# A state-space scan and an FFN on one core: drives on GpSimd and TensorE, decays in SBUF, weighing split between GpSimd and VectorE

## What is computed

```python
x = x + ssm(ctx, layernorm(x), ...)
x = x + ffn(layernorm(x), ...)

def ssm(hidden, z, ...):
    x = einsum('ed,bld->bel', in_proj_w, hidden)
    u = silu(causal_conv4(x) + conv_b)
    dt_lo, Bm, Cm = split(einsum('ke,bel->bkl', x_proj_w, u))
    delta = softplus(dt_proj_w @ dt_lo + dt_proj_b)
    A = -exp(A_log)
    def step(state, ...):                       # over the 256 time steps
        state = state * exp(delta[..., None] * A) + (delta * u)[..., None] * B[:, None, :]
        y = einsum('ben,bn->be', state, C)
    y = (y + D * u) * silu(z)

def bit_linear(x, w, b):                        # the FFN's three products
    x_q = round(x * 127 / max|x|) ; w_q = clip(round(w / mean|w|), -1, 1)
ffn = bit_linear(silu(bit_linear(x, gate)) * bit_linear(x, val), out)
```

## Time and profile before

| | |
|---|---|
| three runs | 226.61, 226.84, 227.04 us (median 226.84) |
| span of the profiled execution | 224.8 us |
| what lies around the span | some 2.0 us (median less span) |
| first scan | 26.94 us |
| last weighing ends | 186.84 us |
| first scan to last weighing | 159.9 us |
| behind the last weighing | 38.0 us |

### The profile page before, as it was taken

One profiled execution on the slowest core, in us unless ns is written; L12 is line 12 of the kernel. 1 busy time (PEld: TensorE's weight loads), 2 busy tenths in 40 slices (PEclk: granted clock), 3 DMA queues, 4 the chain that ended last, 5 costly groups with the idle time before them and its releaser, 6 DMA issues.

```text
span 224.8 us, 2405 instructions
## 1 busy us (share of the span) xinstructions
PE 150.9 (67%) x706; PEld 92.9 (41%) x706; DVE 186.5 (83%) x284; ACT 129.3 (58%) x197; POOL 136.8 (61%) x132
## 2 busy tenths in 40 slices
PE   6983088643979197059630777926986667899983
PEld 5531054232636186048620533504435265334552
DVE  3789999998089999999999968797869998838661
ACT  2578675336585996076341758736498015376772
POOL 5036499778900999896685999999139202691000
PEclk9995559978585769758785596985589969999999
DMA  4894943261400223004003304314000000000002
GB/s 107 231 343 123 339 146 112 87 189 42 140 13 0 75 66 92 4 0 141 0 0 98 135 3 136 73 71 140 23 1 3 23 0 0 0 28 0 23 23 70
DMA packets 12689, 17.44 MB, mean 78 GB/s; under 512 B 3468, under 2 KB 9012, under 8 KB 12678
## 3 DMA queue, kind: packets, MB, share of 16 engines
q1 hardware_dynamic: 12678, 17.30, 24.5%
HBM read 16.11 MB, written 1.19 MB: 77 GB/s over the span
## 4 chain that ended last, share of the span: by engine, by line
DVE 19%; PE 16%; ACT 9%; issue 6%; POOL 5%; DVEq 0%; POOLq 0%; ACTq 0%
DVE wstate L908 3%; PE work L1242 2%; DVE state L898 2%; PE work L1282 2%; DVE gam L981 2%; DVE xhat L825 2%; PE decay L1067 2%; ACT decay L653 2%; DVE pool_state L898 2%; DVE wstage L976 2%; POOL drive L491 2%; ACT gT L722 2%; ACT wstage L703 1%; PE decay L1242 1%; PE work L1249 1%
## 5 line engine op out<-in xcount | busy, mean ns | idle before, releaser
L491 POOL TENSOR_TENSOR drive<-du,b_wide 128x1024 f32<-128x1024 f32 x31 | 74.2, 2407 | 2.9 <-DVE state L898 1.8
L653 ACT ACTIVATE decay<-delta,aneg 128x510 f32<-128x510 f32 x64 | 42.9, 684 | 45.9 <-DVE state L898 23.3
L898 DVE TENSOR_TENSOR_SCAN state<-decay,drive 128x512 f32<-128x512 f32 x44 | 52.4, 1208 | 0.9 <-issue 0.9
L1156 PE MATMUL ysum<-ident,wstate 128*128 128x128 f32 x176 | 32.9, 332 | 10.6 <-DVE wstate L908 10.6
L908 DVE TENSOR_TENSOR wstate<-state,cwide 128x512 f32<-128x512 f32 x44 | 29.1, 663 | 12.2 <-issue 11.8
L1156 PEld LDWEIGHTS ysum<-ident,wstate 128*128 128x128 f32 x176 | 26.1, 172 | 18.8 <-DVE wstate L908 13.8
L501 POOL TENSOR_TENSOR pool_wstate<-pool_state,c_wide 128x1024 f32<-128x1024 f32 x10 | 23.7, 2367 | 11.4 <-PE ysum L1156 8.6
L898 DVE TENSOR_TENSOR_SCAN pool_state<-decay,drive 128x512 f32<-128x512 f32 x20 | 24.3, 1214 | 0.2 <-ACT decay L653 0.2
L1067 PE MATMUL work<-ident,wstage 128*128 128x128 f32 x80 | 14.2, 331 | 11.4 <-ACT ternary L677 7.7
L1177 PE MATMUL cwide<-cparts,sel 128*128 128x512 bf16 x22 | 10.6, 483 | 15.4 <-DVE wstate L908 14.2
L1067 PEld LDWEIGHTS work<-ident,wstage 128*128 128x128 f32 x80 | 11.8, 174 | 12.7 <-ACT ternary L677 8.1
(11 more groups left out here) (180 smaller groups left out, 298.7 us busy)
## 6 DMA issues: line engine op xcount, KB each, us to landing
b_wide<-bc_rows SPq DMA_DIRECT2D x16, 512.0 KB, 4.5
c_wide<-bc_rows SPq DMA_DIRECT2D x10, 256.0 KB, 3.5
x_in<-in_x SPq DMA_DIRECT2D x2, 512.0 KB, 4.9
wstage<-in_L_ffn_gate_w SPq DMA_DIRECT2D x1, 1024.0 KB, 7.8
wstage<-in_L_ffn_val_w SPq DMA_DIRECT2D x1, 1024.0 KB, 10.3
wstage<-in_L_ffn_out_w SPq DMA_DIRECT2D x1, 1024.0 KB, 9.0
ctx_in<-in_ctx SPq DMA_DIRECT2D x2, 256.0 KB, 4.4
out<-wtap SPq DMA_DIRECT2D x4, 128.0 KB, 1.7
```

What stands on the lines that cost most here:

```text
L491: nc.gpsimd.tensor_tensor(drive[:, m % NDR], du[:, m // NS], rows.unsqueeze(1).to_broadcast([P, EH, W]), ALU.mult).then_inc(s_drive, 1)
L653: nc.scalar.activation(v[:, :, 1:L], d[:, :, 1:L], ACT.Exp, scale=aneg[:, eh, n:n + 1]).then_inc(s_decay, 1)
L898: nc.vector.tensor_tensor_scan(dst, decay[i % ND][:], drive[:, i // EH % NDR, i % EH], 0.0, ALU.mult, ALU.add).then_inc(s_scan, 1)
L1156: last = nc.tensor.matmul(ysum[:, k, eh * P:(eh + 1) * P], lhsT=src[:, k * P:(k + 1) * P], rhs=ident[:], start=start and k % LB == 0, stop ...
```

## The change

Almost the whole scan part is written anew; the FFN's products stay.

- The unit of work is a *slot*: a pair of neighbouring states (`NP = 8` pairs a group) of one half of the channels, for both batches. There are 32 slots. Each has two scans, one for each batch, of two states x 256 steps, so again 64 scans of 512 columns.
- `decays` writes SBUF (four slots of buffers), in two activations of 510 columns a slot.
- The drive of three pairs (`DIAG_PAIRS`, 6 slots) comes from TensorE: du is turned (`turn_du`, `duT`), GpSimd writes B on diagonals with an affine select (`diagonals`, `bdiag`), and two fp32 matmuls of 256 columns for each scan put du x B into a PSUM bank. The drive of the other thirteen pairs (26 slots) is a GpSimd multiplication of 1024 columns into SBUF (`pool_drive`, two buffers), two slots ahead.
- C is spread over the partitions by a DMA for every pair (`c_wide`); `spread_c` and `split_c` go. VectorE weighs the 12 slots of `DVE_SLOTS`, GpSimd the other 20, one instruction of 1024 columns each.
- The matrix of the delta projection is multiplied out ahead (`wdT`), so that `pre_delta` needs no copied projection. TensorE adds the parts of softplus (`add_delta`) for three of the four halves. The D x u term is a matmul with a diagonal (`ddiag`).
- silu(layernorm(x)) is one ScalarE activation with scale and bias, turned by TensorE afterwards. The ternary clip is ScalarE's Sign in `weight_rows`; `clip_weights` goes. The two additions of x behind the gate move from GpSimd to VectorE. `scales` is one instruction shorter.
- ctx of group 0 is loaded from ScalarE's queue.

```diff
-NDR = 4
-ND = 3
-POOL_C = (2, 5, 8, 13, 17, 19, 21, 24, 26, 28)
+ND = 4
+NDRV = 4
+NST = 3
+NPW = 2
+NCW = 3
+NBW = 2
+NPD = 2
+DIAG_PAIRS = (0, 1, NP)
+DVE_SLOTS = (3, 5, 7, 9, 11, 13, 15, 17, 19, 21, 23, NSLOT - 1)
+POOL_LEAD = 2
...
+            def load_c(k):
+                if k >= NCW:
+                    for s in slots_of(k - NCW):
+                        wait_weighed(sp, s)
+                sp.dma_start(c_wide[:, k % NCW]..., on_all(1, k)).then_inc(s_cload[k % NCW], 16)
...
+            def diagonals(k):
...
+                nc.gpsimd.affine_select(out=bdiag[:, r % NDG]..., in_=values.unsqueeze(2).to_broadcast([P, GT * 2, P]),
+                                        compare_op=ALU.is_equal, fill=0.0, ...).then_inc(s_diag, 1)
+            def drive_slot(s):
...
+                if r >= NPD:
+                    pool.wait_ge(s_scan, BG * [j for j in range(s) if not on_diag(j)][r - NPD] + BG)
...
+                nc.gpsimd.tensor_tensor(pool_drive[:, r % NPD], rows, b_wide[:, w % NBW], ALU.mult).then_inc(s_pdrive, 1)
+            def weigh(s):
...
+                nc.gpsimd.tensor_tensor(flat(pool_wstate[:, r % NPW]), flat(state[:, s % NST]), flat(c_wide[:, k % NCW]),
                                         ALU.mult).then_inc(s_poolw, 1)
...
+            for s in range(NSLOT):
+                for k in DIAG_PAIRS[2:]:
+                    if s == slots_of(k)[0] - DIAG_LEAD:
+                        diagonals(k)
+                if s + POOL_LEAD < NSLOT and not on_diag(s + POOL_LEAD):
+                    drive_slot(s + POOL_LEAD)
+                if s not in DVE_SLOTS:
+                    weigh(s)
+                if s == POOL_XRSTD:
+                    rstd(0)
...
+                nc.scalar.activation(decay[:, s % ND, :, n, 1:L], d[:, :, 1:L], ACT.Exp,
+                                     scale=aneg[:, eh, 2 * p + n:2 * p + n + 1]).then_inc(s_decay, 1)
...
             def scan(i):
...
+                if on_diag(s):
+                    dve.wait_ge(s_drive, BG * r + b + 1)
+                    rows = drive[(BG * r + b) % NDRV][:]
+                else:
+                    dve.wait_ge(s_pdrive, r + 1)
+                    rows = pool_drive[:, r % NPD, b].rearrange("p n l -> p (n l)")
...
+                nc.vector.tensor_tensor_scan(state[:, s % NST, b]..., decay[:, s % ND, b]..., rows, 0.0,
                                              ALU.mult, ALU.add).then_inc(s_scan, 1)
...
+                nc.vector.tensor_tensor(flat(wstate[:]), flat(state[:, s % NST]), flat(c_wide[:, k % NCW]),
                                         ALU.mult).then_inc(s_wst, 1)
...
+            for i in range(NUNIT):
                 scan(i)
+                if i % BG == BG - 1 and i // BG in DVE_SLOTS:
+                    weigh(i // BG)
+                if i in DVE_XVAR:
+                    k = DVE_XVAR.index(i)
+                    dve.wait_ge(s_x[k // 2], 16)
+                    bn(x_in, 2 * k, 2 * k + 2, s_var if k == 3 else None)
...
+            def drives(i):
...
+                for c in range(LB):
+                    t = b * LB + c
+                    last = nc.tensor.matmul(bank[:, :, c * P:(c + 1) * P], lhsT=duT[:, g, t, eh], rhs=bdiag[:, d % NDG, t],
+                                            start=True, stop=True)
```

More of the change, by code:

```diff
@@ L52 @@
 BROWS = VROW + PARTS * PARTS
[L56 to L68, removed]
@@ L89, in sums_at @@
[L89 to L95, removed]
+NP = NS // 2
+SLOTS = NP * EH
+UNITS = SLOTS * BG
+ORDER = [(0, 0), (1, 0), (0, 1), (1, 1)] + [(p, eh) for p in range(2, NP) for eh in range(EH)]
+NSLOT = G * SLOTS
+NUNIT = G * UNITS
+ND = 4
+NDRV = 4
+NST = 3
+NPW = 2
+NDG = 2
+NCW = 3
+NBW = 2
@@ new lines, with slot_of, slot_parts, slots_of @@
+TURNS, WARM = (6, 6), (16, 3)
+def slot_of(g, p, eh):
+    return g * SLOTS + ORDER.index((p, eh))
+def slot_parts(s):
+    g, k = divmod(s, SLOTS)
+    p, eh = ORDER[k]
+    return g, p, eh
+def slots_of(k):
+    return sorted(slot_of(k // NP, k % NP, eh) for eh in range(EH))
+def pair_of(s):
+    g, p, _ = slot_parts(s)
+    return g * NP + p
+def on_diag(s):
+    return pair_of(s) in DIAG_PAIRS
+def drive_rank(s):
+    return sum(on_diag(k) == on_diag(s) for k in range(s))
+def wide_rank(k):
+    return sum(j not in DIAG_PAIRS for j in range(k))
@@ L1122, in convolve_tap, with pre_delta @@
                     fill(last, name)
+            def pre_delta(g, eh):
+                name = f"pre{g}{eh}"
+                t = work_tile(name)
+                if g == 0:
+                    wait_read(pe, "wd")
+                for k in (1, 0):
+                    wait_u(pe, g, k)
+                    last = nc.tensor.matmul(t[:], lhsT=wdT[:, k, eh * P:(eh + 1) * P], rhs=u[:, k], start=k == 1,
+                                            stop=k == 0)
+                fill(last, name)
             def project(g):
-                name = f"proj{g}"
+                name = f"bc{g}"
                 t = work_tile(name)
@@ L1143, in gates, with turn_b @@
-            def gates(k):
-                name = f"z{k}"
-                t = work_tile(name)
-                pe.wait_ge(s_xhat, LB * (k + 1))
+                for k in (1, 0):
+                    wait_u(pe, g, k)
+                    last = nc.tensor.matmul(t[0:2 * NS, :], lhsT=bcT[:, k], rhs=u[:, k], start=k == 1, stop=k == 0)
+                fill(last, name)
+            def turn_b(g):
+                name = f"bt{g}"
+                t = work_tile(name)
+                wait_read(pe, f"bc{g}")
+                for k in range(GT):
+                    last = turn(t[:, k * NS:(k + 1) * NS], proj[0:NS, k * P:(k + 1) * P])
+                fill(last, name)
@@ new lines, in turn_du, with skips @@
+            def turn_du(g, eh):
+                name = f"dut{g}{eh}"
+                t = work_tile(name)
+                pe.wait_ge(s_du, EH * g + eh + 1)
+                for k in range(GT):
+                    last = turn(t[:, k * P:(k + 1) * P], du[:, g, eh, k * P:(k + 1) * P])
+                fill(last, name)
+            def skips(g):
+                if g:
+                    pe.wait_ge(s_gated, BG * g)
+                else:
+                    pe.wait_ge(s_ddiag, 1)
+                for eh in range(EH):
+                    wait_u(pe, g, eh)
+                    for t in range(GT):
+                        last = nc.tensor.matmul(ysum[:, t, eh * P:(eh + 1) * P], lhsT=u[:, eh, t * P:(t + 1) * P],
+                                                rhs=ddiag[:, eh], start=eh == 0 and t % LB == 0, stop=True,
+                                                skip_group_check=True)
+                last.then_inc(s_skips, 1)
```

944 lines of the change are left out of this document (481 added, 463 removed).

## The result

The changed kernel takes 274.61 us (median of 4 runs, 273.6 to 277.02), the kernel before 226.94 beside it (226.61 to 228.97): ratio 1.2098, 95% interval 1.2021 to 1.2174. It is 21% slower. The forecast was 252 us with a range to 266: the direction and the mechanism hold, the forecast is 22.6 us short, and the time lies 8.6 us beyond the range. The profiled execution took 273.69 us with a span of 271.8, so 1.9 us lie around the span, where 2.0 were taken.

The account below looks back on a forecast made before the run. VectorE was taken to bound the scan stretch before, GpSimd's multiplications plus turns with two-SBUF-input instructions after. 224.8 us of span + 26.5 for a later last weighing - 1 for the tail = 250.3, plus 2.0 gives 252 us; range 236 to 266.

Parts of the forecast that it names:

- Mechanism: Scan stretch: VectorE instructions with two SBUF inputs, scans included, alternate with GpSimd's, each costing GpSimd 0.95 us; main case 0.79.
- Rival A: Scan stretch: scans don't take part in the alternation, 200 us; decides below 0.49 us a scan; chance 0.14.
- Rival C: Whole kernel: nothing gained or lost, the start's 4.2 us and fewer waits meeting a scan price near 0.5; chance 0.02.
- The sum: Whole kernel: GpSimd's instructions plus turns, 4 us of waits, FFN work at nothing; span 250.3, time 252 us.
- rival B: Slots 20 to 31: VectorE's FFN work is not covered, 15 us and small ones more, 272 us; chance 0.05.
- Start, first scan at 22.7: Before the scans: shorter ScalarE chain and no C split bring the first scan to 22.7, gaining 4.2 us (bounds 0 and 5).
- a first scan later than 27: Start: a first scan later than 27 us was named as a sign that the forecast is wrong.
- Slots 0 to 4, end at 44.2: First slots: statistics end near 34, GpSimd's rstd at 36.4, drive of slot 4 at 39.7, its last scan at 44.2.
- Slots 5 to 23, 120.2 us: Middle slots: GpSimd's multiplications 68.4, VectorE's turns 41.8, other work 6, waits about 4 us, ending at 164.4.
- Slots 24 to 31, 48.9 us: Last slots: multiplications 30.7, scans 13.3, residual 2.9, last slot 2 us, FFN work at nothing, ending at 213.3.
- Tail, 37.0: After the last weighing: shorter scales and an addition no longer against GpSimd's take 1 us off 38.0.
- What the profile should have shown: Scans on SBUF drives near 3 us, GpSimd's drives and weighings 3.0 to 3.3, VectorE's weighings 2 to 3, GpSimd over 85% busy.

Follow-up runs that it names:

- Run 1: Changed kernel with its 52 scans on GpSimd drives reading a PSUM bank instead, GpSimd still making every drive: 240.98 us, 1.0661 to the kernel before.
- run 2: The kernel before with only its decays moved from PSUM to SBUF: 280.73 us, ratio 1.2464.
- run 4: Changed kernel with the scans of slots 24 to 31 alone (16 of 52) reading their drive from PSUM: 266.12 us, 1.1779 to the kernel before.
- Run 5: Changed kernel with TensorE's first drives ahead of du's second half, which goes behind scan 1: 276.12 us, 1.2231 to the kernel before.
- Run 3: Changed kernel with the scans of slots 4 to 15 alone (24 of 52) reading their drive from PSUM: 254.71 us, 1.128 to the kernel before.
- run 6: Changed kernel with rstd for x and two other pieces of GpSimd's small work moved back: 272.84 us, 1.2084 to the kernel before.
- run 11: Changed kernel, 52 scans reading PSUM drives, GpSimd's drives not waiting for scans, second VectorE result buffer for one drive buffer: 232.63 us, 1.0282 to the kernel before.
- run 7: Changed kernel with all sixteen pairs' drives made by TensorE: 237.41 us, 1.0535 to the kernel before.

## Why the prediction missed, step by step

**Mechanism: right.** GpSimd and VectorE take turns for whole instructions, and the scan takes part as soon as its second input is in SBUF. Runs 1 and 2 show it from both sides. Rival A had its condition at under 0.49 us for each scan; the turns cost 0.65 in this kernel and 0.87 in the kernel before, and even without them (241) the change is slower. Rival C needed a scan price near 0.5 and a start gain of 4.2, and had neither.

**The sum: failed where it lets GpSimd run without waiting.** It adds GpSimd's instructions and turns, with 4 us of waits, and costs VectorE's FFN work for group 0 at nothing. Run 1 splits it. Without the turns of the scans the kernel takes 241 us, not 200: 41 us of waits and of a later start that the sum doesn't have. The turns add 34 us to that, not 52: 18 too many; that a turn which falls into a wait costs less than 0.95 would explain them (run 4). The forecast is 22.6 us short and not 41 because these two misses offset each other, which is luck. So is the nearness to rival B's 272, which had 15 us of VectorE's own work in it. The steps, one after the other:

**Start, first scan at 22.7: failed.** It came at 29.26, outside the bounds of 0 to 5 us of gain. I had ended the sum at the first du; in the changed order TensorE turns the second half of du ahead of the first drives, and the first scan waits for these (1.77 us for L1252). Run 5 shows that this alone is worth nothing. The forecast had named a first scan later than 27 as a sign that it is wrong.

**Slots 0 to 4, end at 44.2: failed.** Slot 4's second scan ended near 52.9. The statistics ended at 40.4, where 34 was written, `rstd` took 3.4 us with four small operations for the 2.4 counted, and the drive behind it ended at 46.24 for 39.7. Then slot 4's first scan, begun at 46.32, came 0.13 us behind the start of a weighing (46.19) and waited for all of it, where I had put it ahead. The step named the right chain. 8.7 of the 21.5 us that the span is over the forecast arise up to here.

**Slots 5 to 23, 120.2 us: near as a sum, its terms less so.** They took 124.6 (52.9 to 177.5). GpSimd's stretched instructions and its waits for scans make 39.7 us there by the groups by line ((3023 - 2360) x 18 + (3073 - 2360) x 10 = 19.0, and 16.1 + 4.6), where 45.8 were counted. Against it stand 8.0 us of one wait for the layer norm's statistics of group 0, 2.2 for a scale, and 12.4 us of small work, where 6 were counted: small operations are stretched as well. 4.4 us more in all; one drive of the 29 multiplications had already run, and the last one ends 2.2 us behind 177.5. These are terms of GpSimd's time and not yet prices at the end. Run 3 prices the turns of slots 4 to 15 at 0.83, and run 6 gives back under 2 us for shorter waits.

**Slots 24 to 31, 48.9 us: failed at the FFN cost of nothing.** They took 54.9. VectorE's FFN work was put at nothing because it would run in GpSimd's time. Its waits don't run there; whether its work does, no run separates. The timeline has VectorE idle 4.31 us for a product (L1335) at 187.32, and 1.61 and 3.44 us for two more (L1371). While it stands, no scan is made, and GpSimd stands behind (L520 waits 6.9 us for scans here). TensorE itself was at a granted clock of 0.63 in this stretch, where the nearest rows of before have 0.77. This is near rival B, with waits for TensorE in place of VectorE's own 15 us. In run 1 this stretch takes 47.7 us, where rival A's sum had 35.6, so 12 us of it don't come from turns at all; the turns were over-priced here (0.53 by run 4). 6.0 us more.

**Tail, 37.0: 39.4.** The shorter scale operations were there, and the tail grew, so an expected gain of 1 became a loss of 1.4 in all against 38.0. Why is open; TensorE's granted clock in it was 0.96 for 1.00. These four stretches are 8.7 + 4.4 + 6.0 + 2.4 = 21.5 us, the whole of 271.8 - 250.3.

**What the profile should have shown.** VectorE's weighings at 2.13 (2 to 3) fit, and drives and weighings of GpSimd at 2.95 and 2.90 us lie just under the 3.0 to 3.3. The scans' mean of 2.11, and a median of 1.34, do not fit "near 3": about half of them hardly wait. GpSimd busy over 85% does not fit either (75%). That was the sign that the sum took for one busy engine what are two that wait for each other and for TensorE.

**What stays open.** Run 1 lies 41 us over the 200 of rival A. By its own times: the first GpSimd drive at 43.5 for 36.4 (7), slots up to 23 in 108.6 for 88.7 (20), slots 24 to 31 in 47.7 for 35.6 (12), the tail in 39.9 for 37 (3). Of these the result buffer accounts for some 9 (run 11). That the rest is round trips with TensorE, at its lower clock, and the statistics is read from waits. No run takes the FFN of group 0 out of the stretch, so its share is argued and not shown.

## What to carry to other kernels

Before an operand of VectorE moves from PSUM to SBUF, count the instructions that then have two SBUF inputs beside a busy GpSimd: the move alone cost this kernel 55.7 us for 64 scans, 0.87 each. When two engines feed each other through one or two buffers and take turns too, the work of the busier engine is not the time: without the scans' turns this kernel stood 41 us over that sum, and a move of work (with a result buffer) that looked like a gain of 6 to 12 us lost 5. Price the turns and the waits apart, by a run without the turns. Take the parts of a large change one by one: three small ones of this one, put alone into the kernel before, made it 4.9% faster, while the whole was 21% slower.

## What was not expected of the hardware

Small instructions are stretched by turns as well. GpSimd's tensor-scalar of 128x4 (L476) took 1.01 us beside VectorE and its 128x8 form 0.20 beside a scan that reads its drive from PSUM; an affine select of 128x1024 (L505) took 2.08 us beside VectorE and 1.09 at the start. VectorE's normalising with a single SBUF tensor, 128x256 and two columns of scalars, also took long beside GpSimd: 7.44 us for four, and 4.15 in the kernel before, where GpSimd multiplied too; the shortest single one took 388 ns. GpSimd's three multiplications beside these four kept their 2.3 to 2.4 us. The runs do not show why:

```profile
150.62 7.44 DVE L890 TENSOR_SCALAR mag<-lnw,mv,nv 128x256 f32<-128x256 f32 x4 [0.86 <-POOL nv L477]
```

TensorE's granted clock over a whole execution was 0.79 in the changed kernel with TensorE busy 66%, and 0.94 with sixteen pairs, where it was busy 84%. The drives as matmuls in run 7 ran at 400 ns each for 403 in the changed kernel, though five times as many.
